# A four-layer graph network on one core: 23 row gathers of the PNA and GATv2 passes move from GpSimd's indirect DMAs to row-by-row fetches of SyncE

## What is computed

```python
# _L2_gnn_ref (PNA), N = 6250 nodes, E = 100000 edges, 128 features
m = jnp.concatenate([h[dst], h[src]], axis=-1) @ W_pre + b_pre
mean = jax.ops.segment_sum(m, dst, num_segments=n) / deg
mean_sq = jax.ops.segment_sum(m * m, dst, num_segments=n) / deg
mn = jnp.where(has, jax.ops.segment_min(m, dst, num_segments=n), 0.0)
mx = jnp.where(has, jax.ops.segment_max(m, dst, num_segments=n), 0.0)
# _L3_gnn_ref (GATv2)
h = x_l[src] + x_r[dst]
h = jnp.where(h >= 0, h, NEG_SLOPE * h)
e = h @ att
e_max = jax.ops.segment_max(e, dst, num_segments=n)
alpha = jnp.exp(e - e_max[dst])
denom = jax.ops.segment_sum(alpha, dst, num_segments=n)
out = jax.ops.segment_sum(alpha[:, None] * x_l[src], dst, num_segments=n)   # alpha divided by denom[dst]
# the network: four residual layers
x = x + gat(h); x = x + gcn(h); x = x + pna(h); x = x + gatv2(h)            # h = relu(layernorm(x)) before each
```

## Time and profile before

| What | Value |
|---|---|
| median of 3 runs | 4626.91 us (4619.5 to 4628.82) |
| the profiled execution | 4617.97 us, its span 4615.9 us |
| busy in the span | PE 3159.7 (68%), PE weight loads 2667.1 (58%), DVE 3209.7 (70%), ACT 2334.3 (51%), POOL 3221.9 (70%) |
| PNA gathers | 2275.5 to 3250.6 us |
| GATv2 gathers | 3523.1 to 4565.3 us |

### The profile page before, as it was taken

One profiled execution on the slowest core, in us unless ns is written; L12 is line 12 of the kernel. 1 busy time (PEld: TensorE's weight loads), 2 busy tenths in 40 slices (PEclk: granted clock), 3 DMA queues, 4 the chain that ended last, 5 costly groups with the idle time before them and its releaser, 6 DMA issues. The chain is left out here.

```text
span 4615.9 us, 79158 instructions
## 1 busy us (share of the span) xinstructions
PE 3159.7 (68%) x19497; PEld 2667.1 (58%) x19497; DVE 3209.7 (70%) x7496; ACT 2334.3 (51%) x4887; POOL 3221.9 (70%) x3428
## 2 busy tenths in 40 slices
PE   4888888887633334334566666666696888888886
PEld 3666666665533333334455555555465777777776
DVE  5888888888633333334689898989656766667667
ACT  4766666665300000000677777777436666666665
POOL 4777777776577777777677777777315777777774
PEclk7555555555765666655788888888897888888887
DMA  7333333332122222221388888888623333333332
GB/s 140 89 89 86 88 87 89 87 88 61 48 55 55 56 56 55 56 57 51 114 291 290 286 290 289 296 283 295 200 76 87 83 80 82 80 80 82 82 80 76
DMA packets 368300, 567.20 MB, mean 123 GB/s; under 512 B 107029, under 2 KB 171192, under 8 KB 367861
## 3 DMA queue, kind: packets, MB, share of 16 engines
q1 hardware_dynamic: 254190, 332.06, 22.5%
q0 software_dynamic: 106720, 227.64, 20.2%
q10 hardware_dynamic: 6950, 2.44, 0.2%
...
## 5 line engine op out<-in xcount | busy, mean ns | idle before, releaser
L896 POOL DMA_INDIRECT e_G<-dr_tab,src_idx x830 | 792.7, 955 | 272.4 <-issue 233.5
L896 POOL DMA_INDIRECT v_G<-dr_tab,src_idx x830 | 790.3, 952 | 253.3 <-issue 247.4
L2123 POOL DMA_INDIRECT m_G<-dr_tab,chunk_src x782 | 738.0, 944 | 247.1 <-issue 238.0
L1899 POOL DMA_INDIRECT s_G<-dr_tab,chunk_src x760 | 717.5, 944 | 235.6 <-issue 226.5
L2007 PE MATMUL s_OUT<-s_G,s_S 128*128 x1664 | 375.3, 416 | 560.5 <-POOLq L1892 525.3
L2007 PEld LDWEIGHTS s_OUT<-s_G,s_S 128*128 128x128 f32 x1664 | 349.9, 320 | 585.6 <-issue 585.6
L1953 DVE TENSOR_TENSOR ACC<-ACC,s_OUT 128x129 f32 x832 | 241.3, 290 | 592.1 <-PE s_OUT L2007 475.7
L2269 PE MATMUL m_BK<-eye,m_XT 128*128 128x128 f32 x3136 | 492.5, 310 | 155.1 <-ACT m_XB L2182 149.8
L2182 ACT COPY m_XB<-m_BK 128x512 f32<-128x512 f32 x784 | 428.0, 592 | 276.1 <-PE m_BK L2269 275.1
L2269 PEld LDWEIGHTS m_BK<-eye,m_XT 128*128 128x128 f32 x3136 | 408.3, 161 | 230.5 <-issue 187.6
L1329 PE MATMUL e_OUT<-e_RH,e_S 128*128 128x144 f32 x1664 | 511.9, 476 | 1.9 <-DVE e_RH L1215 1.9
...
## 6 DMA issues: line engine op xcount, KB each, us to landing
...
e_LR<-dr_row_loc SPq DMA_DIRECT2D x104, 256.0 KB
v_LR<-dr_row_loc SPq DMA_DIRECT2D x104, 256.0 KB
...
s_G<-dr_tab SPq DMA_DIRECT2D x1408, 0.5 KB
s_G<-dr_tab ACTq DMA_DIRECT2D x1408, 0.5 KB
e_G<-dr_tab,src_idx POOLq DMA_INDIRECT x830
v_G<-dr_tab,src_idx POOLq DMA_INDIRECT x830
```

The source lines that it names most:

```text
L896: pool.indirect_dma_start(out=out, out_offset=None, in_=table, in_offset=bass.IndirectOffsetOnAxis(ap=g["src_idx"][:, step:step + 1], axis ...
L1899: pool.indirect_dma_start(out=G[:, c % (RING * GROUP), 0:D], out_offset=None, in_=table[:, :], in_offset=bass.IndirectOffsetOnAxis(ap=g["c ...
L2123: pool.indirect_dma_start(out=G[:, k % Q, c % GROUP, :], out_offset=None, in_=table[:, :], in_offset=bass.IndirectOffsetOnAxis(ap=g["chunk ...
```

## The change

In each of 11 PNA groups (k = 10, 18, ... 90) and 12 GATv2 groups (k = 11, 19, ... 99) POOL leaves the eighth gather out. The 128 rows of that chunk or step are fetched by SP, 16 rows in each of the eight groups ahead, into a buffer `GX` of two halves. In PNA, SP handles them in groups 0 to 87, in GATv2 in groups 2 to 97. The source numbers lie on one partition (`INDEX`); DVE once multiplies them by the bytes of a row, and SP loads 16 into registers and issues 16 DMAs of 512 B (PNA) or 516 B (GATv2). For GATv2, whose steps are not the chunks, the numbers of all steps are stored to HBM in the preamble (`step_src`, 448 KB). PE, ACT and DVE read the eighth chunk's rows from `GX`; PE waits for them. The core of the diff, GATv2's part first, then PNA's:

```diff
+PIECE = 16
+PNA_FETCHED = [k * GROUP + GROUP - 1 for k in range(10, PICKS - 2, P // PIECE)]
+V_FETCHED = [k * GROUP + GROUP - 1 for k in range(11, GROUPS - 3, P // PIECE)]
...
+        ("step_src", (SPAD, P), I32),
...
+                sp.dma_start(g["step_src"].rearrange("(k p) e -> p k e", p=P), edges[:, :, 0:P]).then_inc(rows_out, 16)
...
-                sp.wait_ge(rows_out, 64)
+                sp.wait_ge(rows_out, 80)
...
+def load_places(nc, places, row):
+
+    _, vals = nc.values_load_multi_w_load_instructions(
+        places, engines=[mybir.EngineType.SP], min_val=0, max_val=(N - 1) * row,
+        skip_runtime_bounds_check_because="the sources are numbers of nodes, here times the bytes of a row")
+    return vals
...
+        GX = sb("GX", [P, 2, AC + 1])
+        INDEX = sb("INDEX", [1, len(V_FETCHED), P], I32)
+        table_bytes = table.bitcast(U8).rearrange("(o r) b -> o (r b)", o=1)
...
+        def gathers(k):
+            return [t for t in range(k * GROUP, min((k + 1) * GROUP, REAL_STEPS)) if t not in V_FETCHED]
+
+        def landings(k):
+            return 16 * sum(len(gathers(j)) for j in range(k % 4, k + 1, 4))
+
+        def number(k):
+            return V_FETCHED.index(k * GROUP + GROUP - 1) if k * GROUP + GROUP - 1 in V_FETCHED else None
+
+        def row(k, s):
+            n = number(k)
+            return GX[:, n % 2, :] if n is not None and s == GROUP - 1 else G[:, k % 4, s, :]
...
+                pool.memset(GX[:, :, 0:1], 1.0).then_inc(start, 1)
                 for k in range(GROUPS):
                     b = k % 4
                     for s in range(GROUP):
+                        if k * GROUP + s in V_FETCHED:
+                            continue
...
                     sp.dma_start(LR[:, c, :], g["row_loc"][bass.ds(k * SLOTS, SLOTS)].partition_broadcast(P)).then_inc(locrow_in[c], 16)
+                    n, p = (k - 2) // (P // PIECE), (k - 2) % (P // PIECE) * PIECE
+                    if 0 <= n < len(V_FETCHED):
+                        if k == 2:
+                            sp.wait_ge(index_bytes, 1)
+                        places = load_places(nc, INDEX[:, n, p:p + PIECE], 4 * AC)
+                        if p == 0 and n >= 2:
+                            sp.wait_ge(rh_done, V_FETCHED[n - 2] + 1)
+                        for u, place in enumerate(places):
+                            sp.dma_start(GX[p + u:p + u + 1, n % 2, 1:AC + 1].bitcast(U8),
+                                         table_bytes[:, bass.ds(place, 4 * AC)]).then_inc(fetched[n % 2], 16)
                     wait(sp, drop_done, k - 1)
...
+                for n, t in enumerate(V_FETCHED):
+                    sp.dma_start(INDEX[:, n, :], g["step_src"][t:t + 1, :]).then_inc(index_in, 16)
...
-                        nc.scalar.activation(RH[:, s, :], G[:, b, s, 0:AC], ACT.Copy, scale=PW[:, s:s + 1]).then_inc(rh_done, 1)
+                        nc.scalar.activation(RH[:, s, :], row(k, s)[:, 0:AC], ACT.Copy, scale=PW[:, s:s + 1]).then_inc(rh_done, 1)
...
+                dve.wait_ge(index_in, 16 * len(V_FETCHED))
+                V.tensor_single_scalar(INDEX[:], INDEX[:], 4 * AC, op=ALU.mult).then_inc(index_bytes, 1)
...
+                    n = number(k)
+                    if n is None:
+                        V.tensor_tensor(cols[:], columns, G[:, b, :, D + 1], ALU.add).then_inc(cols_in, 1)
+                    else:
+                        last = GROUP - 1
+                        V.tensor_tensor(cols[:, 0:last], columns[:, 0:last], G[:, b, 0:last, D + 1], ALU.add)
+                        V.tensor_tensor(cols[:, last:GROUP], columns[:, last:GROUP], GX[:, n % 2, D + 1:D + 2], ALU.add).then_inc(cols_in, 1)
...
+                    n = number(k)
+                    if h == 1 and n is not None:
+                        pe.wait_ge(fetched[n % 2], 16 * P * (n // 2 + 1))
                     for s in range(h * HALF, (h + 1) * HALF):
-                        ins = nc.tensor.transpose(GT[:, s * P:(s + 1) * P], G[:, b, s, 1:D + 1], g["eye"][:])
+                        ins = nc.tensor.transpose(GT[:, s * P:(s + 1) * P], row(k, s)[:, 1:D + 1], g["eye"][:])
...
+        lo = PARTS * D
+        GX = fin.spare[:, lo:lo + 2 * D].rearrange("p (b d) -> p b d", b=2)
+        INDEX = fin.spare[0:1, lo + 2 * D:lo + 2 * D + len(PNA_FETCHED) * P].bitcast(I32).rearrange("o (n e) -> o n e", e=P)
+        table_bytes = table.bitcast(U8).rearrange("(o r) b -> o (r b)", o=1)
...
+        def gathers(k):
+            return [c for c in range(k * GROUP, min((k + 1) * GROUP, CHUNKS)) if c not in PNA_FETCHED]
+
...
+        def rows_of(k):
+            return G[:, k % Q], (PNA_FETCHED.index(k * GROUP + GROUP - 1) if k * GROUP + GROUP - 1 in PNA_FETCHED else None)
...
-                    for c in range(k * GROUP, min((k + 1) * GROUP, CHUNKS)):
+                    for c in gathers(k):
...
+                for n, c in enumerate(PNA_FETCHED):
+                    sp.dma_start(INDEX[:, n, :], src[c * P:(c + 1) * P].unsqueeze(0)).then_inc(index_in, 16)
...
+                sp.wait_ge(index_bytes, 1)
                 for k in range(PICKS):
                     if 1 <= k and k + 3 < PICKS:
                         sp.wait_ge(scanned, PARTS * k)
                         same(k + 3)
+                    n, p = k // (P // PIECE), k % (P // PIECE) * PIECE
+                    places = load_places(nc, INDEX[:, n, p:p + PIECE], 4 * D) if n < len(PNA_FETCHED) else []
+                    if places and p == 0:
+                        wait(sp, gt_done, PNA_FETCHED[n - 2] // GROUP + 1 if n >= 2 else 0)
+
+                    def fetch(some):
+                        for u in some:
+                            if places:
+                                sp.dma_start(GX[p + u:p + u + 1, n % 2, :].bitcast(U8),
+                                             table_bytes[:, bass.ds(places[u], 4 * D)]).then_inc(fetched[n % 2], 16)
+                    fetch(range(0, 4))
                     for q in range(PAIRS):
+                        if q:
+                            fetch(range(4 * q, 4 * q + 4))
                         sp.wait_ge(xb_done, halves(k, PARTS - 1) + q // 2 + 1)
                         sp.dma_start(rows[:, k * GROUP + 2 * q + 1:k * GROUP + 2 * q + 3, :],
                                      XB[:, k % 2, 2 * q:2 * q + 2].rearrange("p s m d -> p s (m d)")).then_inc(stored[k % 2][q], 16)
...
+                dve.wait_ge(index_in, 16 * len(PNA_FETCHED))
+                V.tensor_single_scalar(INDEX, INDEX, 9, op=ALU.logical_shift_left).then_inc(index_bytes, 1)
...
+                    rows, n = rows_of(k)
+                    if n is not None:
+                        pe.wait_ge(fetched[n % 2], 16 * P * (n // 2 + 1))
                     for s in range(GROUP):
-                        ins = nc.tensor.transpose(GT[:, k % 2, s * P:(s + 1) * P], G[:, k % Q, s, :], g["eye"][:])
+                        row = GX[:, n % 2, :] if n is not None and s == GROUP - 1 else rows[:, s, :]
+                        ins = nc.tensor.transpose(GT[:, k % 2, s * P:(s + 1) * P], row, g["eye"][:])
```

More of the change, by code:

```diff
@@ L13 @@
 import math
-F32, I32, BF16 = mybir.dt.float32, mybir.dt.int32, mybir.dt.bfloat16
+F32, I32, BF16, U8 = mybir.dt.float32, mybir.dt.int32, mybir.dt.bfloat16, mybir.dt.uint8
 ALU, ACT, AX = mybir.AluOpType, mybir.ActivationFunctionType, mybir.AxisListType
@@ L1429, in gatv2_pass @@
         masks_in = [sem(f"masks_in{c}") for c in range(2)]
+        index_in = sem("index_in")
+        index_bytes = sem("index_bytes")
+        fetched = [sem(f"fetched{b}") for b in range(2)]
         whole_in = sem("whole_in")
@@ L1600, in _ @@
                 dve.wait_ge(whole_in, 16)
-                dve.wait_ge(start, 6)
+                dve.wait_ge(start, 7)
                 def larger(k, h):
@@ L1648, in columns_out @@
                     dve.wait_ge(columns_done, k + 1)
-                    V.tensor_tensor(cols[:], columns, G[:, b, :, D + 1], ALU.add).then_inc(cols_in, 1)
+                    n = number(k)
[5 more added lines that the diff above has]
+                        V.tensor_tensor(cols[:, last:GROUP], columns[:, last:GROUP], GX[:, n % 2, D + 1:D + 2], ALU.add).then_inc(cols_in, 1)
                 def factors_of_nodes(k, b):
@@ L1768, in _ @@
                 tiles = tiles_of(0)
-                pe.wait_ge(start, 6)
+                pe.wait_ge(start, 7)
                 for h in range(2):
@@ L2051, in factors_of_counts, with moments_pass @@
         dve.wait_ge(chain, 3)
-def moments_pass(nc, g, table, extremes, fin):
+def moments_pass(nc, g, table, extremes, fin, src):
     name = "m_"
@@ L2109, in moments_pass @@
         xb_done = sem("xb_done")
+        def gathers(k):
+            return [c for c in range(k * GROUP, min((k + 1) * GROUP, CHUNKS)) if c not in PNA_FETCHED]
         def landings(k):
-            return 16 * (min((k + 1) * GROUP, CHUNKS) - k * GROUP + k // Q * GROUP)
+            return 16 * sum(len(gathers(j)) for j in range(k % Q, k + 1, Q))
```

(8 more changed lines are left out.)

## The result

| | before | after |
|---|---|---|
| median of four executions, us | 4624.8 (4619.5 to 4628.8) | 4700.3 (4697.3 to 4705.8) |
| span of the profiled execution, us | 4615.9 | 4697.5 |

The ratio is 1.0161 (95% interval 1.0149 to 1.0174): the change makes the kernel 75 us slower. The forecast was 4604.3 us in a range of 4592 to 4630, and it was wrong. SyncE became the bound of the PNA pass, as in the prediction's first rival, and beside it the gain in GATv2 stayed away.

A forecast was written before the change was run, and what follows sets the result against it. POOL's gathers were taken as the bound in PNA and GATv2. Terms -13.7 - 15.0 + 1.0 + 0.2 (memset) + 2.3 + 1.6, written as -22.6 us, took 4618.0 to 4595.4, median 4604.3 (8.9 above); range 4592 to 4630.

The forecast's parts named there:

- What bounds the kernel before: PNA and GATv2: POOL's gathers, one every 1.249 us without a stop, set the pace; the whole saving should show.
- SP's fetches in PNA: SP's loop in PNA: 9.2 us a group with fetches, under POOL's 9.83, so price 0.
- Rival 1: PNA: SP becomes the bound at 10.8 us a group, +71 us, a median of 4688; chance 0.12.
- Rival 2: PNA: transfers set the pace, so moving an issue gains nothing and the 13.7 us stay, 4618; chance 0.08.
- rival 3: PNA: one DMA engine carries all rows, +62 at 0.13 us a row, a median of 4680; chance 0.03.
- GATv2's loop: GATv2's groups: 12 gathers fewer save 15.0 us; SP's loop, at most 8.8 us, stays under 8.99, price 0.
- +1.0 for holds: GATv2's gathers: groups already disturbed can lose part of their 1.249 us, +1.0 us (0 to 3).
- The start of GATv2: DVE's split waits for 12 loads and starts 8.5 us late; POOL stops, +2.3 us (0 to 6.8).
- Preamble: Before the passes: storing step_src, 448 KB, while DMA is full costs +1.6 us (0 to 2.5).
- Start of PNA: Ahead of DVE's preparation: loads, landing and shift take 6.4 us, hidden in DVE's idle 12.13 us.
- The sum: Whole kernel: the terms of both passes and the preamble, written as -22.6 us, giving a median of 4604.3 us.

The follow-up runs named there:

- e3: Changed kernel with PNA's part alone and 8 rows a group instead of 16, five chunks fetched: 4612.7 us, 0.9985 of the kernel before.
- e10: Changed kernel with PNA's part alone and 12 rows a group instead of 16, eight chunks fetched: 4609.8 us, 0.9977 of the kernel before.
- e5: Changed kernel with PNA's part alone, 16 numbers loaded once ahead of the loop, the same 16 rows fetched every group: 4610.2 us, 0.9961 of the kernel before.
- e12: Kernel before, all gathers kept, but in 88 PNA groups SP loads 16 numbers and issues only the last row: 4625.5 us, ratio 0.9999.
- e2: Changed kernel with PNA's part alone, GATv2 as before and step_src not stored: 4697.7 us, 1.0168 of the kernel before.
- e4: Changed kernel with GATv2's part alone, loads of numbers ahead of whole, multiplication behind the split: 4603.4 us, 0.9969 of the kernel before.
- e1: Changed kernel with GATv2's part alone, POOL gathering all 782 PNA chunks: 4618.1 us, 0.9996 of the kernel before.
- e7: Changed kernel with GATv2's part alone, loads of numbers ahead of whole, multiplication left ahead of the split: 4617.1 us, 0.9976 of the kernel before.
- e11: Changed kernel with 12 PNA rows a group, GATv2's loads of numbers ahead of whole, multiplication behind the split: 4596.9 us, 0.9951 of the kernel before.
- e9: Kernel before plus PNA's number loads, shift and unused register loads, which the trace lacks; no rows issued: 4620.0 us, ratio 1.0000.

## Why the prediction was wrong, step by step

- **What bounds the kernel before: right.** POOL was the bound, and 1.249 us is the worth of a gather: e3, e10 and e5 gained 6.9, 10.1 and 17.7 us for 5, 8 and 11, by the sum 6.2, 10.0 and 13.7.
- **SP's fetches in PNA: here it failed.** The prediction gave SP 9.2 us a group against POOL's 9.83; it is 10.96. Term by term: the rows 5.8 predicted and 6.09 measured, stores with `SAME` 2.5 and, with the gaps between, 0.46 + 1.56 + 0.54 = 2.56, the register load 0.9 and 2.31. Of the missing 1.76 us the load is 1.41. The 0.9 was an estimate that added 0.12 us to the median of eight numbers in GCN, a quiet pass. Sixteen take 1.16 in GATv2, and 2.10 here. The prediction had looked for the queueing in the stores and in `SAME`, took it to be "gone" with the burst, and had not asked whether a register load would wait too. That the load tips it is shown by e5; that it waits for the stores' queueing fits e12 and the trace, but is not shown by itself. The margin was 0.63 us: one term off by more than that turned the sign.
- **Rival 1: this is what happened.** It said 10.8 us a group, 88 x 0.81 = +71 us, 4688. Measured: 88 x (10.96 - 9.99) = +85, less what the last ten groups, which have no fetches, win back. DVE's scans of one kind stand 8.95 us apart there (3298.17, 3307.12, 3316.07), 1.04 under 9.99, so 10.4 us, and +75 remain; the stretches say 56.3 + 20.3 = 76.6, e2's median 78. The rival's reason ("nothing of the queueing is saved") was right in the sum though not in the place: the stores were rid of it, the load and the rows were not. With 0.9 for the load and 0.36 a row its 10.8 lies this close to 10.96 in part by luck, since its 4.1 for stores and `SAME` was an upper bound and they take 2.56. A chance of 0.12 was too little for a sum whose margin was smaller than the distance between its own bounds (a row at 0.36 or 0.42 alone makes 1.0 us a group).
- **Where the loss shows.** The prediction would have looked for it in the gathers' span alone. A quarter of it, 19.3 us, comes behind the last gather, because POOL's ring had filled.
- **Rival 2 and rival 3: not so.** If DMA had been the limit, no gather taken from POOL would have gained; each did. The Trainium skill, "DMA: Bandwidth & Descriptors", section "Issuing engines are not separate DMA queues", calls the sequencer time that several issuing engines save usually small. In this case it is the whole matter, 1.249 us a gather at POOL and 10.96 us a group at SP. One DMA engine as the carrier of all rows would have held e5, which fetches 16 rows in each group and runs at POOL's pace. The price of a packet there came from 6950 packets of a queue in the whole execution; in GCN that queue has 3414. It changes nothing in the outcome.
- **GATv2's loop: no cost, as predicted, but one term stood for nothing.** SP's waits from 4000 to 4100 us of the changed kernel, and one gather in POOL's timeline of the kernel before:

```profile
SPq L1559 <- DVE v_drop L1693: 19.4, 10, 2.5
```
```profile
3573.01 0.94 POOL L896 DMA_INDIRECT v_G<-dr_tab,src_idx  x1 [0.30 <-DVE ACC L1670]
```

  SP waited 79.2 us of 100 for `drop` before, so its own work is now about 7.9 us a group (8.8 predicted), under cover. e4's gathers span 15.3 us less, for 15.0 predicted. The +1.0 for holds was a misreading: the 5.0 us "held up by others" in the earlier trace rows are the usual 0.30 us between two gathers, put down to DVE in some of them. No gather of the pass stands more than 0.37 us behind the one before it, before or in e4.
- **The start of GATv2: the slack was right, the delay was not.** Predicted: 12 x 0.30 = 3.6 us of issue and a split 8.5 us late. The 0.30 came from GCN, where nothing strided was queued ahead. Behind `whole` they cost 0.83 each and landed later (3.5 us to DVE's start, 1.5 predicted), and the split came 16.8 us late. Instead of +2.3 us the term was +11.4, beyond its upper bound of 6.8. With the longer gathers (2.0 us in e1), which the prediction did not have, it ate nearly all of the pass's 15.0.
- **Preamble: too small to see.** +1.6 was predicted. In the executions with gathers at 944 ns, PNA's first gather comes between 2274.1 and 2277.9 us with the store (e1, e4, e7, e11) and between 2273.0 and 2280.9 without it (before, e2, e3, e5, e9, e10). A cost of 1.6 us is neither shown nor excluded.
- **Start of PNA: right**, 0 (e9).
- **The sum.** -13.7 - 15.0 + 1.0 + 0.2 + 2.3 + 1.6 is -23.6 and not the -22.6 written, so the forecast by its own terms was 4603.3 us. Against a miss of 96 us that is nothing.
